# Layer 1's attention of a group moved half a turn later in a two-layer graph network on one core

## The reference

```python
def layer0(x, adj, ...):                  # per graph: x 128 x 256, adj 128 x 128
    nx = ln(x, ln1_g, ln1_b)
    q, k, v = nx @ wq + bq, nx @ wk + bk, nx @ wv + bv         # 8 heads of 32
    bias = where(adj > 0, 0.1 * adj * adj, -inf)
    p = softmax(q @ k.T / sqrt(32) + bias)
    x1 = x + (p @ v) @ wo + bo
    return x1 + gelu(ln(x1, ln2_g, ln2_b) @ w1 + b1) @ w2 + b2  # w1 256 x 1024, w2 1024 x 256

def layer1(x, adj, ...):
    s = (x @ Wq) @ (x @ Wk).T / 16
    w = softmax(where(adj == 0, -inf, s))
    return ln(x + (w @ (x @ Wv)) @ Wo + bo, gamma, beta)
```

## Time and profile before

| | us |
|---|---|
| median of 3 runs (lowest, highest) | 935.13 (934.89, 935.47) |
| the profiled execution | 935.03 |
| its span, from first to last instruction | 933.3 |
| TensorE busy | 903.3 (97%) |
| VectorE busy | 691.0 (74%) |
| ScalarE busy | 641.2 (69%) |
| GpSimd busy | 388.6 (42%) |

### The profile page before, as it was taken

The page is one execution under the profiler, slowest core; times in us unless marked ns, Lnnn a source line. Parts: engine busy times, 40 slices in busy tenths (PEclk is TensorE's granted clock), DMA queues, the critical chain, the costliest instruction groups (busy, mean ns, idle before and its releaser), DMA issues.

```text
span 933.3 us, 22588 instructions
## 1 busy us (share of the span) xinstructions
PE 903.3 (97%) x7623; PEld 805.8 (86%) x7623; DVE 691.0 (74%) x2576; ACT 641.2 (69%) x1888; POOL 388.6 (42%) x257
## 2 busy tenths in 40 slices
PE   8889999999999999999999999999999999998995
PEld 8677798988889898888989888898988889898894
DVE  7676877869587786958779595877968687786745
ACT  5675958668496766858677585866758586685751
POOL 3425153543616354262535526263451626344221
PEclk9999999999999999999999999999999999999998
DMA  7101000010101001010100101010010100000001
GB/s 260 35 1 35 2 24 24 30 29 0 56 0 34 22 22 34 0 51 6 34 22 22 34 0 35 22 34 22 22 34 0 34 22 28 11 24 1 24 1 34
DMA packets 29727, 26.29 MB, mean 28 GB/s; under 512 B 1126, under 2 KB 29436, under 8 KB 29692
## 3 DMA queue, kind: packets, MB, share of 16 engines
q1 hardware_dynamic: 29676, 25.83, 8.8%
q10 hardware_dynamic: 16, 0.00, 0.0%
HBM read 17.44 MB, written 8.39 MB: 28 GB/s over the span
## 4 chain that ended last, share of the span: by engine, by line
PE 43%; issue 21%; DVE 15%; POOL 14%; ACT 6%; POOLq 1%; DVEq 0%; ACTq 0%
PE bank L327 10%; PE bank L329 9%; PE bank L328 9%; DVE nx L1083 4%; POOL x L1519 4%; DVE hT_lo L1009 3%; PE bank L471 3%; POOL y L1524 3%; PE bank L564 3%; PE bank L592 3%; ACT bank L829 2%; PE bank L463 2%; POOL adj_s L1468 2%; POOL bias L1477 2%; POOL rstd L1450 2%
## 5 line engine op out<-in xcount | busy, mean ns | idle before, releaser
L804 ACT ACTIVATE bank<-p_s,neg_max 128x128 f32<-128x128 f32 x512 | 182.2, 356 | 24.1 <-DVE neg_max L1112 23.9
L1450 POOL TENSOR_TENSOR rstd<-ve,minus_half 128x4 f32<-128x4 f32 (+1 forms) x51 | 54.9, 1077 | 312.8 <-DVE ve L1076 312.8
L327 PE MATMUL bank<-w_hi,hT_hi 128*128 128x256 f32 x512 | 147.4, 288 | 0.0
L329 PE MATMUL bank<-w_hi,hT_lo 128*128 128x256 f32 x512 | 144.1, 282 | 0.0
L328 PE MATMUL bank<-w_lo,hT_hi 128*128 128x256 f32 x512 | 144.1, 281 | 0.0
L1112 DVE CUSTOM_DVE_ANT_0 p_s<-bank,bias 128x128 f32<-128x128 f32 x512 | 112.5, 285 | 8.4 <-PE bank L463 8.3
L327 PE MATMUL bank<-n2T_hi,w_hi 128*128 128x512 f32 (+1 forms) x272 | 110.1, 405 | 3.4 <-DVE qk_lo L1010 3.3
L829 ACT ACTIVATE bank<-bank,vec_cols 128x512 f32<-128x512 f32 (+1 forms) x136 | 86.6, 637 | 30.5 <-PE bank L329 30.5
L329 PE MATMUL bank<-n2T_hi,w_lo 128*128 128x512 f32 (+1 forms) x272 | 104.0, 382 | 0.0
L328 PE MATMUL bank<-n2T_lo,w_hi 128*128 128x512 f32 (+1 forms) x272 | 103.8, 382 | 0.0
L327 PEld LDWEIGHTS bank<-w_hi,hT_hi 128*128 128x128 f32 x512 | 96.4, 188 | 2.5 <-DVE hT_lo L1009 0.8
(11 more groups left out here) (211 smaller groups left out, 2460.4 us busy)
## 6 DMA issues: line engine op xcount, KB each, us to landing
xs<-in_x SPq DMA_DIRECT2D x15, 512.0 KB, 3.7
out<-y SPq DMA_DIRECT2D x15, 512.0 KB, 2.9
adj_i<-in_adj SPq DMA_DIRECT2D x15, 256.0 KB, 2.8
x2T_f<-in_L_gnn_w SPq DMA_DIRECT2D x1, 512.0 KB, 7.0
tT<-in_L_gnn_w SPq DMA_DIRECT2D x1, 512.0 KB, 7.8
y<-in_L_gnn_w SPq DMA_DIRECT2D x1, 512.0 KB, 6.4
vo<-in_L_gnn_w SPq DMA_DIRECT2D x1, 512.0 KB, 7.8
x_bo<-in_x SPq DMA_DIRECT2D x1, 256.0 KB, 2.8
```

The source lines that it names most:

```text
L327: mm(out, a_hi, b_hi, start=first, stop=False)
L329: return mm(out, a_lo, b_hi, start=False, stop=last)
L804: last = run(bank[r][:, NODES * place:NODES * place + NODES], p_s[:, r, place, :], ACT.Exp, scale=-1.0, bias=neg_max[:, r, place:place + 1 ...
L1450: P.tensor_tensor(t["rstd"][:, 0:k], t["ve"][:, 0:k], minus_half[:, 0:k], ALU.pow).then_inc(ln_pool[n], 1)
```

## The change

Layer 1's attention of a group no longer ends in the group's own turn. A fourth group, gc = gb - 1, is handed to TensorE's and ScalarE's turns. On TensorE `p1_transpose(gc)` stands right behind the transposes of ga's p for pair 0 and writes bank 0, one of the four banks that these have just written; so it waits until ScalarE's `pT_copy(ga, 0, 0)` has emptied that bank. `attend1(gc)` stands right behind `attend(ga, 0)` and writes banks 2 and 3; before `attend` TensorE waits for `p1T_copy(gc)`. `scores(ga, 1)` waits for `residual3(gc)`, since it writes banks 2 and 3 again.

On ScalarE `exps1(gb)` moves behind the sixteen `exps(gp, 0, r)` at the end of the turn, `p1T_copy` moves to the next turn behind `pT_copy(ga, 0, 2)`, and the copy of vo that ScalarE made goes to VectorE, which now copies both halves. On VectorE `inverse_sums1` and `residual3` move to the middle of the next turn's MLP, and `sums3`, `moments3` and `norm3` to its second half; GpSimd's `rstd(3)`, `gain` and `offset` follow them. Group 15 keeps its former banks and, with group 16, its place in `last_turn`. Number and size of the instructions on TensorE stay as they were; no DMA is added, the store of a group is issued later.

```diff
-        p1_bank, av1_bank, n2_bank = 4, (6, 7), (6, 7)
+        p1_bank, av1_bank, n2_bank = 0, (2, 3), (6, 7)
...
             def scores(g, q):
...
+                if q == 1 and not (isinstance(g, int) and g == 1):
+                    pe.wait_ge(dve_y, graph0(g - 1))
...
-            def attend(g, q):
+            def attend(g, q, gc=None):
+                if gc is not None:
+                    pe.wait_ge(act_p1T, gc + 1)
                 pe.wait_ge(act_pT, 2 * (pair0(g) + q) + 2)
...
             def mlp_up(g, j, A):
...
-                elif j == 0:
-                    pe.wait_ge(act_p1T, g)
                 elif j == 1 and A:
                     pe.wait_ge(act_v, pair0(g + 1) + size(g + 1) // 2)
...
                 elif j == 3:
-                    pe.wait_ge(dve_y, graph0(g))
+                    pe.wait_ge(dve_vo, pair0(g))
...
-            def p1_transpose(g):
+            def p1_transpose(g, ga=None):
+                if ga is not None:
+                    pe.wait_ge(act_pT, 2 * pair0(ga) + 1)
                 pe.wait_ge(act_p1, graph0(g) + size(g))
...
-            def turn(gp, ga, gb):
-                P, A, B = gp is not None, ga is not None, gb is not None
+            def turn(gp, ga, gb, gc):
+                P, A, B, C = gp is not None, ga is not None, gb is not None, gc is not None
...
                 if A:
                     p_transpose(ga, 0)
+                if C:
+                    p1_transpose(gc, ga)
                 if B:
                     mlp_up(gb, 4, A)
                 if A:
-                    attend(ga, 0)
+                    attend(ga, 0, gc)
+                if C:
+                    attend1(gc)
...
                     for q in pairs(gb):
                         vo_project(gb, q, A)
-                    p1_transpose(gb)
...
                     project_v(gp, 1)
-                if B:
-                    attend1(gb)
...
-            def turn(gp, ga, gb):
+            def turn(gp, ga, gb, gc):
...
                 if A:
                     pT_copy(ga, 0, 0)
                     pT_copy(ga, 0, 2)
+                if C:
+                    p1T_copy(gc)
...
-                if B:
-                    exps1(gb)
                 if P:
                     exps(gp, 0, 0)
-                if B:
-                    vo_copy(gb)
-                    p1T_copy(gb)
-                if P:
                     exps(gp, 0, 1)
+                    exps(gp, 0, 2)
                     if size(gp) > 2:
                         v_copy(gp, 1)
-                    exps(gp, 0, 2)
                     exps(gp, 0, 3)
+                if B:
+                    exps1(gb)
...
                     h_low(gb, 3)
+                if C:
+                    inverse_sums1(gc)
+                    for q in pairs(gc):
+                        residual3(gc, q)
...
                     pT_copy(ga, 1, 1)
                     pT_copy(ga, 1, 3)
+                if C:
+                    sums3(gc)
+                    moments(3, gc)
+                if A2:
                     attn_low(ga, 1)
...
                 if B:
                     t_copy(gb)
+                if C:
+                    norm3(gc)
```

More of the change, by code:

```diff
@@ L191, in at @@
         def at(n, g):
+            if n == "p1" and isinstance(g, int) and g == GROUPS - 2:
+                return 4
+            if n == "av1" and isinstance(g, int) and g == GROUPS - 2:
+                return (6, 7)
             if n == "n2" and isinstance(g, int) and g == 0:
@@ L586, in attend1 @@
                 pe.wait_ge(act_p1T, g + 1)
-                pe.wait_ge(act_vo, g + 1)
-                if size(g) > 2:
-                    pe.wait_ge(dve_vo, g)
+                if is_last(g):
+                    pe.wait_ge(act_vo, 2)
+                elif isinstance(g, int) and g == GROUPS - 2:
+                    pe.wait_ge(act_vo, 1)
+                    pe.wait_ge(dve_vo, pair0(g) + 1)
+                else:
+                    pe.wait_ge(dve_vo, pair0(g + 1))
                 for q in pairs(g):
@@ L733, in _ @@
             l1_product(0)
-            turn(2, 1, 0)
-            turn(3, 2, 1)
+            turn(2, 1, 0, None)
+            turn(3, 2, 1, 0)
             with pe.Fori(3, GROUPS - 2) as g:
-                turn(g + 1, g, g - 1)
-            turn(GROUPS - 1, GROUPS - 2, GROUPS - 3)
-            last_turn(GROUPS - 1, GROUPS - 2)
+                turn(g + 1, g, g - 1, g - 2)
+            turn(GROUPS - 1, GROUPS - 2, GROUPS - 3, GROUPS - 4)
+            last_turn(GROUPS - 1, GROUPS - 2, GROUPS - 3)
         @block.scalar
@@ L1315, in turn @@
                     biased(gp, 0, 2)
-                if B and size(gb) > 2:
-                    vo_copy(gb)
-                if P:
-                    biased(gp, 0, 3)
-                if B:
-                    inverse_sums1(gb)
-                if P:
-                    divided(gp, 0, 0)
                 if B:
                     for q in pairs(gb):
-                        residual3(gb, q)
+                        vo_copy(gb, q)
                 if P:
-                    divided(gp, 0, 1)
-                    divided(gp, 0, 2)
-                    divided(gp, 0, 3)
+                    for r in range(3, HPT):
+                        biased(gp, 0, r)
+                    for r in range(HPT):
+                        divided(gp, 0, r)
             def last_turn(ga, gb, gc):
-                sums3(gc)
                 h_low(gb, 0)
@@ L1341, in last_turn @@
                 h_low(gb, 3)
-                norm3(gc)
+                inverse_sums1(gc)
+                for q in pairs(gc):
+                    residual3(gc, q)
                 residual1(ga, 0, True)
@@ L1537, in turn @@
                     pool.wait_ge(ln_dve[1], ln_end(gp))
-                if C:
-                    gain(gc, size(gc))
-                    offset(gc, size(gc))
-                if P:
                     adjacency(gp)
@@ L1544, in turn @@
                     bias(gp)
+                if C:
+                    rstd(3, gc)
                 if B:
@@ L1551, in turn @@
                     x_plus_bo(gp)
+                if C:
+                    gain(gc, size(gc))
+                    offset(gc, size(gc))
                 if A:
```

42 lines of the change are left out of this document (20 added, 22 removed).

## The result

| | before | after |
|---|---|---|
| time, median (n = 4 each, same chip) | 935.18 us (934.89 to 935.47) | 974.48 us (972.39 to 974.97) |
| ratio after/before, 95% interval | | 1.0416 (1.0398 to 1.0434) |
| profiled execution, its span | 935.03, 933.3 | 974.17, 972.4 |
| TensorE busy in the steady stretch | 742.72 of 746.00 | 748.03 of 778.00 |
| a turn, from one scores(gp, 0) to the next | 54.92 | 57.40 |

The change makes the kernel 4.2% slower, the forecast was 972.5. In this document's names S is again the start of scores(gp, 0). The code's lines have moved: 327 to 329 are now 331 to 333 (products), 463 is 469 (scores), 471 is 477 and 582 is 594 (transposes of p and of layer 1), 482 is 490, 592 is 608 (attend1); on ScalarE 804 is 823, 810 is 829, 853 is 872, 862 is 881, 869 is 888; on VectorE 1083 is 1101, 1112 is 1130.

A forecast was written before the change was run, and what follows sets the result against it. TensorE's list bounds the kernel; the moved transposes make it wait for ScalarE's copy of p. 32.8 + 1.3 + 0.9 + 0.8 + 1.7 = 37.5 on 935.03 gives 972.5 us, range 962 to 982.

The forecast's parts named there:

- TensorE's list is the turn, and moving work along it is worth nothing by itself: TensorE, steady turn: its list sets the turn and its sum stays; only new waits count.
- The first exponential at S + 2.40, the chain of 12.17 to the copy of p: ScalarE behind the scores: layer 0's exponentials start at S + 2.40, the copy of p starts 12.17 later, at S + 14.57.
- The first piece, 15.68: TensorE from S to the MLP's product j = 4 of the next turn: 15.68 instead of 14.89, 0.79 more.
- The pause of 2.4, some of it at j = 1: TensorE idles 2.4 before layer 1's transposes, perhaps partly at the MLP's product j = 1, waiting for the copy of v.
- The second piece, +1.73: TensorE from product j = 4 to the next S: grows by attend1's 1.73.
- A steady turn, +2.52: Both pieces of a steady turn: 0.79 + 1.73 = 2.52 more; 13 pairs between turns 2 and 15 give 32.8.
- Turn 1 to 2, +1.33 and +0.86: Group 0 has two graphs: first piece 14.69 against 13.36, 1.33 more; its product in turn 2 adds 0.86.
- Turn 15 to the end, +0.79 and +1.73: From turn 15 to 16 the first piece adds 0.79; group 14's product in turn 16 adds 1.73.
- rival B: A 2.4 pause every turn lowers TensorE's granted clock: 24 more if in 14 turns, about 996; 5%.
- VectorE at zero: VectorE's moved norm and residual work fits its idle time: zero, with 0.3 a turn as upper bound.
- Rival A: ScalarE's later p1T copy delays avT_hi, avT_lo and output projection: 0.6 to 1 more in 15 turns, 982 to 988; 7%.
- Rival C: ScalarE is quicker, copy of p 1 to 2 us earlier: turn grows only 0.6 to 1.5, 944 to 958; 5%.

The follow-up runs named there:

- the change with ScalarE short enough: Changed kernel with layer 1's exponentials first, Exp in place of Gelu (no table loads), copy of v behind eight exponentials instead of twelve: 934.87 us, 0.9985.
- the unchanged order without table loads: Kernel before with Exp in place of Gelu, so no table loads: 934.95 us, ratio 0.9976.
- the kernel without tables: Changed kernel with layer 1's exponentials ahead of layer 0's and Exp in place of Gelu, copy of v still behind twelve exponentials: 953.30 us, 1.0195.
- the run where the copy of t took that room: Changed kernel with VectorE's copy of t ahead of the normalisation of x1: 972.75 us, ratio 1.0389.
- the one with y's normalisation early: Changed kernel with VectorE's copy of t ahead of the normalisation of x1 and y's normalisation ahead of both: 968.10 us, ratio 1.0321.

## Why the prediction was right

- **TensorE's list is the turn, and moving work along it is worth nothing by itself.** Shown: the change with ScalarE short enough runs at 0.9985 of before, the unchanged order without table loads at 0.9976. The first piece of a turn is there 431.24 − 418.09 = 13.15, and the forecast's list without a wait was 12.74 + 0.42 = 13.16.
- **The first exponential at S + 2.40, the chain of 12.17 to the copy of p.** Measured 2.39 and 12.16.
- **The first piece, 15.68.** Measured 15.69, with two small errors that took each other out: the transposes start at S + 15.29 instead of 15.16 (the first copy of p ends at 449.60 + 0.54 = 450.14, so the hand-over is 0.20 and not 0.05), and from there to j = 4 it is 0.40 and not 0.10 + 0.42.
- **The pause of 2.4, some of it at j = 1.** Measured 442.71 − 441.66 − 0.23 = 0.82 there and 450.34 − 446.99 − 1.66 = 1.69 before the transposes, 2.51 in all (the idle times in brackets, 0.66 and 1.44, leave out the modelled ends of the records ahead). The size was right; that the forecast treated the first as a detail was not. In the kernel without tables, where it is 0.4 longer and stands alone, it is worth the 2.1% between 1.0195 and 0.9985.
- **The second piece, +1.73.** Measured 57.40 − 15.69 = 41.71 against 54.92 − 14.89 = 40.03, 1.68.
- **A steady turn, +2.52.** Measured 2.48. Thirteen of them are 32.8 forecast and, with the 2.4 of turn 14, 32.2 measured.
- **Turn 1 to 2, +1.33 and +0.86.** Measured 1.2 together: this step was 1.0 too large. The first piece grew by 1.17 (14.53 against 13.36), the second by 0.03 and not by 0.86. Before the change TensorE waited in turn 2 for VectorE's low part of attention's output, and this wait is not there after it, since group 0's product now lies ahead of that place; the term had added the product and not looked for a wait that it fills:

```profile
110.35 0.39 PE L327 MATMUL bank<-wo_hi,avT_hi 128*128 128x256 f32 x1 [0.56 <-DVE avT_lo L1009]
```

- **Turn 15 to the end, +0.79 and +1.73.** Measured 3.8, so the forecast was 1.3 too small. The first piece grew by 0.50 (15.04 against 14.54) and not by 0.79; the rest is rival B, which came true once and cost 1.5 (below).
- **Not in the sum at all:** 1.9 at the start of the program. In the stretch from 9 to 14 us the granted clock is 0.66, where it was 1.00 before, with the same list of instructions on TensorE. The first scores of the program then start at 14.97 instead of 13.07. The kernel before with Exp in place of Gelu shows the same (0.66, and 14.96), so it does not come from the change. Without it the longer span is 37.2, and the forecast's terms gave 37.5; that the sum is so close is partly luck, since turn 1 to 2 came out 1.0 too large and the end 1.3 too small.
- **VectorE at zero.** Right for the time, and idle time was the reason given; but the forecast did not see that one of the four moved normalisations would grow from 0.4 to 2.1 us. That this just fitted was luck: the normalisations end at 433.71 and the next instruction starts at 433.70, where VectorE idled 2.96 us before the change. In the run where the copy of t took that room a turn lost 0.53, more than the upper bound of 0.3.
- **Rival A** did not come: attend at 452.31 follows the j = 4 product by 1.57, as before (1.56), and no wait behind the transposes is longer.
- **Rival C** did not come by itself, since the list had no hole; made by hand (layer 1's exponentials first) it is worth 18 us.
- **What the profile was to show:** busy 748.03 of 778.00 is 96% (95% forecast); turns of 57.40 (57.4); ScalarE idle for 3.28 (about 3); an idle time before the transposes of 1.44 in brackets and 1.69 between the starts (1.5 to 2.4); the granted clock of 1.00 over the steady stretch. Only the last turn departs from it.

Rival B in the last turn, TensorE in order of time and then busy time by stretch (the last three numbers are the granted clock, DMA share and GB/s):

```profile
902.22 1.91 PE L477 MATMUL bank<-ident,p_s 128*128 128x128 f32 x16
907.22 0.66 PE L594 MATMUL bank<-ident,p 128*128 128x128 f32 x4 [3.09 <-ACT pT L829]
...
910.26 1.55 PE L490 MATMUL bank<-pT,v 128*32 128x128 f32 x32
```

```profile
907.00:912.00 5.00, 4.78 (x43) 3.50 (x44) 1.70 (x3) 4.65 (x10) 0.00 (x0) 0.66 0.00 0
112.00:890.00 778.00, 748.03 (x6308) 663.08 (x6307) 600.92 (x2149) 524.70 (x1536) 322.05 (x205) 1.00 0.07 21
```

The pause is 3.09 there, and behind it six products take 2.63 instead of 1.57 and attend 1.49 instead of 1.01: 1.5 us, and the clock is at 0.66 in the five us that hold it, with 1.00 in the five before. The pauses of the steady turns, 1.44 beside 0.66, left it at 1.00. Rival B was priced with 1.7 for a fall, and 5% for it to happen in all turns; one turn was never among its cases.

## What to carry to other kernels

On an engine that is busy all the time and works in order, moving work matters only through the waits at the new place. Find the other engine's list that ends there, see whether the moved work was what gave it time, and give that engine its own idle hole first. Look for a second wait almost as long before you price the removal of the first: here answering the one before the transposes alone gave half of the loss back, and answering the other alone then gave nothing. And an instruction that waits for a third engine should not stand ahead of one that TensorE needs first, even if the second becomes ready a little later (the copy of tT, 0.8% for one moved line in the kernel before); look whether the delayed one has idle time to pay with, for in the kernel after it had none.

## What the runs showed of the hardware

**A VectorE normalisation is held while GpSimd adds.** In the kernel after, VectorE and GpSimd in one turn:

```profile
430.05 0.68 DVE L1199 COPY tT<-bank 128x512 f32<-128x512 f32 x1
430.65 3.06 DVE L1101 TENSOR_SCALAR y<-y,mv,rstd 128x256 f32<-128x256 f32 x4
...
433.70 1.29 DVE L1027 TENSOR_TENSOR n2T_lo<-bank,n2T_hi 128x512 fp32r<-128x512 f32 x2
```

```profile
430.21 2.38 POOL L1519 TENSOR_TENSOR x_bo<-xs,bo_r 128x1024 f32<-128x1024 f32 x1 [1.61 <-DVE nx L1101]
433.80 2.36 POOL L1540 TENSOR_TENSOR y<-y,gamma_r 128x1024 f32<-128x1024 f32 x1 [1.20 <-DVE y L1101]
```

The first of the four, taken alone:

```profile
430.65 2.10 DVE L1101 TENSOR_SCALAR y<-y,mv,rstd 128x256 f32<-128x256 f32 x1
```

It ends at 432.75, 0.16 behind the addition (430.21 + 2.38 = 432.59), and the three behind it take 0.40 each. In the run with the copy of t first, the one that meets the addition lasts from 430.97 to 433.44, and the addition ends at 433.29. So it lasts as long as the addition does. The copy from PSUM beside the same addition takes its usual 0.68, and the two instructions for n2T_lo, which read PSUM, take 1.29 for the two beside GpSimd's next multiplication, no more each than the copy's 0.68. Nor are all instructions between tiles in SBUF held: in the kernel before two sums of a norm (BATCH_NORM_STATS2, x to stats) start at 392.31 and take 0.74 beside GpSimd's multiplication (392.56 to 394.96), and the normalisations of y take 1.38 for four beside GpSimd's small rstd (128x4, from 386.00). The Trainium skill, Advanced Engine Details and Errata, "VectorE Performance Modes", says that VectorE's second SBUF port is shared with GpSimd and that VectorE's two-port instructions and GpSimd's block each other, and that this mode is for source and destination in SBUF. The trace agrees in that a normalisation between tiles in SBUF is held and instructions that read PSUM are not; the sums of a norm and the small rstd show that SBUF at both ends is not enough. That the port is the cause was not tested by itself. What the runs show is that the time goes away when the normalisations no longer meet the addition (mean 794 to 408 ns).

**The length of a pause does not decide whether the granted clock falls behind it.** The longest pause, 3.3 us near 52 us, is in all 13 traces with a fall right behind it. The pause of 3.09 in turn 16 is in three: the clock fell behind it in the kernel after and in the one with y's normalisation early, and stayed at 1.00 in the one with the copy of t alone moved, with the same pause of 3.09 at 907.00:

```profile
907.00:912.00 5.00, 5.00 (x51) 4.05 (x52) 1.49 (x3) 4.65 (x9) 0.00 (x0) 1.00 0.00 0
```

A pause of 1.8, a wait for the copy of tT in turn 15, is in eight traces, and the clock fell behind it in three of them. One is the kernel with layer 1's exponentials first:

```profile
873.75 0.38 PE L331 MATMUL bank<-nxT_hi,wq_hi 128*128 128x256 f32 x1 [1.79 <-DVE tT L1199]
```

```profile
874.00:878.00 4.00, 4.00 (x23) 4.00 (x23) 2.93 (x6) 1.67 (x3) 2.80 (x2) 0.57 0.00 0
```

And at the start of the kernel after it fell with no pause near it (0.66 from 9 to 14 us, TensorE busy 5.00 of 5.00). The pauses of 1.4 in the steady turns never took it down.

**What stays open:** why the granted clock in the first 14 us differs between executions of nearly the same program, why it falls behind one pause and not behind its equal in another run, and whether the port is what holds the normalisation.
